# Two P times V back to back every eight tiles, scores in stretches of three, in a fused attention and gated-adapter kernel

## The reference

```
xn = layernorm(x)
q = (xn @ Wq.T + bq) * scaling              # 16 heads x 16
k, v = split(xn @ Wkv.T + bkv)              # one head of 16 each
w = softmax(qr @ k.T)                       # per batch 16*512 rows, 512 keys
attn = (w @ v) @ Wo.T + bo
...
logits = x @ w_gate                         # adapter: best of 6 experts by gate
attn = softmax(x @ tokens.T * C ** -0.5)
delta = ((attn @ val + x) @ wd_w.T + wd_b) * scale
out = log(sum(exp(delta) * gates))
...
x = x + attn_branch(xn) + ffn_branch(xn)
```

## Time and profile before

| | |
|---|---|
| Median of 3 runs | 902.43 us (899.44 to 903.38) |
| The profiled execution | 902.32 us, its span 900.4 us |
| PE busy | 857.9 us, 95% of the span |
| DVE busy | 780.2 us, 87% |
| ACT busy | 674.6 us, 75% |
| POOL busy | 512.7 us, 57% |
| Chain that ended last | PE 79%, DVE 15%, issue 3% |

### The profile page before, as it was taken

The page is one execution under the profiler, slowest core; times in us unless marked ns, Lnnn a source line. Parts: engine busy times, 40 slices in busy tenths (PEclk is TensorE's granted clock), DMA queues, the critical chain, the costliest instruction groups (busy, mean ns, idle before and its releaser), DMA issues.

```text
span 900.4 us, 17856 instructions
## 1 busy us (share of the span) xinstructions
PE 857.9 (95%) x5913; PEld 288.0 (32%) x5913; DVE 780.2 (87%) x1489; ACT 674.6 (75%) x1370; POOL 512.7 (57%) x691
## 2 busy tenths in 40 slices
PE   7779999999999999999999999999999999999988
PEld 5332232323323232332323333233333323232223
DVE  7698898989989898998989898898989889898935
ACT  3117887877878787787878778787787878887884
POOL 3764566665556666565666656566664656635210
PEclk8688999999999999999999999999999999999999
DMA  4431343434344343534435353443435334241212
GB/s 129 105 69 37 105 81 95 108 101 119 85 107 101 97 112 97 118 86 118 89 97 113 96 119 85 118 95 92 113 95 119 85 118 92 74 111 50 63 59 72
DMA packets 125073, 86.06 MB, mean 96 GB/s; under 512 B 57143, under 2 KB 109112, under 8 KB 124984
## 3 DMA queue, kind: packets, MB, share of 16 engines
q1 hardware_dynamic: 124824, 84.82, 38.2%
q10 hardware_dynamic: 160, 0.10, 0.0%
HBM read 39.30 MB, written 33.54 MB: 81 GB/s over the span
## 4 chain that ended last, share of the span: by engine, by line
PE 79%; DVE 15%; issue 3%; ACT 1%; POOL 1%; DMA 1%; SPq 0%; DVEq 0%
PE pO L373 25%; PE pA L355 19%; DVE M L829 9%; PE pB L360 8%; PE pA L496 5%; PE pA L443 5%; PE pA L514 4%; PE pA L498 3%; PE pA L432 2%; PE pA L468 2%; PE pA L483 2%; DVE st L749 2%; PE pB L476 1%; ACT P L648 1%; PE pB L454 1%
## 5 line engine op out<-in xcount | busy, mean ns | idle before, releaser
L829 DVE TENSOR_REDUCE M<-pA 128x1 f32<-128x512 f32 x1024 | 651.9, 681 | 80.1 <-PE pA L355 76.0
L648 ACT ACTIVATE P<-pB 128x512 f32<-128x512 f32 x1002 | 555.4, 603 | 133.2 <-PE pB L360 129.6
L355 PE MATMUL pA<-K,Q 48*128 48x512 f16 x1024 | 324.6, 388 | 25.1 <-DVE M L829 9.8
L360 PE MATMUL pB<-Q,K 50*128 50x512 f16 x1002 | 317.5, 385 | 0.3 <-DVE M L829 0.3
L373 PE MATMUL pO<-P,VK 128*32 128x512 f32 x2048 | 273.5, 606 | 2.1 <-ACT OTr L654 1.1
L355 PEld LDWEIGHTS pA<-K,Q 48*128 48x128 f16 x1024 | 67.8, 94 | 344.7 <-DVE M L829 285.1
L975 POOL TENSOR_SCALAR Cz<-Cx 128x512 f32<-128x512 f32 x32 | 62.1, 1941 | 38.6 <-ACT Cx L630 38.6
L373 PEld LDWEIGHTS pO<-P,VK 128*32 128x32 f32 x2048 | 40.5, 108 | 99.2 <-issue 66.2
L514 PE MATMUL pA<-wo,On 128*128 128x256 f32 x246 | 70.2, 407 | 0.0
L360 PEld LDWEIGHTS pB<-Q,K 50*128 50x128 f16 x1002 | 64.0, 94 | 7.4 <-ACT P L648 5.5
L960 POOL TENSOR_SCALAR Ms<-M 128x32 f32<-128x32 f32 x32 | 9.7, 303 | 97.5 <-DVE M L829 97.5
(11 more groups left out here) (156 smaller groups left out, 807.8 us busy)
## 6 DMA issues: line engine op xcount, KB each, us to landing
o_parts<-OTr SPq DMA_DIRECT2D x62, 256.0 KB, 2.3
X<-in_x SPq DMA_DIRECT2D x16, 512.0 KB, 3.9
q_pieces<-Qp SPq DMA_DIRECT2D x64, 128.0 KB
out<-OUT SPq DMA_DIRECT2D x32, 256.0 KB, 3.4
Op<-o_parts SPq DMA_DIRECT2D x31, 256.0 KB
Rb<-l_parts SPq DMA_DIRECT2D x31, 256.0 KB
Q<-q_pieces SPq DMA_DIRECT2D x30, 256.0 KB, 4.5
Q<-q_pieces SPq DMA_DIRECT2D x34, 128.0 KB, 4.6
```

The costliest lines, as they stand in the source:

```text
L355: e.matmul(bank1("ab", t)[:, :], Q16[r:r + 48, b % 3, h, 128 * s:128 * s + 128], K16[r:r + 48, b % 3, :], start=True, stop=True).then_inc( ...
L360: e.matmul(bankB(t)[:, :], K16[r:r + 50, b % 3, 128 * i:128 * i + 128], Q16[r:r + 50, b % 3, :, 32 * hh:32 * hh + 32], start=True, stop=Tr ...
L648: e.activation(P[:, u % PR, :], bankB(u + LB)[:, :], ACT.Exp, scale=alpha).then_inc(S("e"))
L829: e.tensor_reduce(M[:, t // 32 % 2, t % 2, t % 32 // 2:t % 32 // 2 + 1], bank1("ab", t)[:, :], AX, ALU.max, negate=True).then_inc(S("mx"))
```

## The change

The distance of P times V, the stretches of pairs and the ring are changed, in `slots()` and one constant:

```diff
-PR = 12
+PR = 16
...
     for n in range(NT + LB):
-        put("ab", n - n % 2 + 0.02 * (n % 2) if n < NT else n - n % 4 + 0.02 * (n % 4), n)
+        put("ab", n - n % 8 + (0, 0.02, 0.04, 3.3, 3.32, 3.34, 6, 6.02)[n % 8] if n < NT else n - n % 4 + 0.02 * (n % 4), n)
...
     for v in range(NT // 4):
-        put("pv", 4 * (v + LV + (v + LV >= NT // 4)) + 1, v)
+        if v + LV < NT // 4:
+            put("pv", 8 * ((v + LV) // 2) + 5.6 + 0.1 * (v % 2), v)
+        else:
+            put("pv", 4 * (v + LV + (v + LV >= NT // 4)) + 1, v)
```

## The result

The changed kernel takes **1008.79 us** (median of 4, 1006.19 to 1010.44) against 900.93 us for the kernel before in the same session: ratio 1.119, 95% interval 1.117 to 1.121. The forecast was 971 us in a range of 924 to 1000. The sign held, and so did the waits that it worked out; the clock, which it had put at nothing, is what takes the time out of the range.

The account below looks back on a forecast made before the run. PE bounds the kernel: 50.5 us a batch without waits, less 1.9 for joins, plus 8.4 of bank waits gives 57.0 against 52.39. Over about 14.5 batches +67, last batch +2: 902.3 + 69 = 971 us, range 924 to 1000.

Parts of the forecast that it names:

- What bounds the kernel, and the joins: PE sets the pace, 50.5 us a batch without waits; joining two P times V saves 1.9 us a batch.
- Stretches of three and fillers in pB: The third score pair behind five pB fillers a batch waits for a conversion on ACT: 5.3 us a batch.
- What comes on top, worked: Further bank waits in the filler windows, worked: 3.1 of 8.4 us, giving a batch of 57.0 us.
- From a batch to the kernel: About 14.5 batches, 4.6 us more each: +67 us; start and tail within 3 us, last batch +2.
- The clock falls: PE at half clock around the L461 window in a third to all batches: 990 to 1020 us, chance 0.15.
- Its price: Cost of the clock falling: 3.5 us at half clock, 1.2 to 3.5 us a batch, 990 to 1020 us.
- The rule named beside that rival: Skill text: PE idling briefly between matmul groups cycling through banks swings the clock; by it, falling clock would be the forecast.
- The smaller rival: Only the five pB filler waits count, slack takes up the rest: 53.9 us a batch, 925 us, chance 0.14.
- the faster one: pB banks come back in time, so only the joined P times V count: 875 us, chance 0.04.
- The ring at nothing: P gets 16 slots in place of 12 for the later P times V; costed at nothing.

Follow-up runs that it names:

- e1: The changed kernel with the four conversions of pB fillers moved on ACT ahead of the exponential of the tile following the filler: 941.1 us, ratio 1.044.
- e3: Only the stretches of three, three and two, with P times V one by one as in the kernel before: 976.8 us, ratio 1.083.
- e11: The changed kernel with 2 to 4 extra matmuls over all 128 rows in PE's holes ahead of five pairs a batch: 977.7 us, ratio 1.085.
- e6: The changed kernel with the ring of exponentials at 12 slots, as before the change: 1009.5 us, ratio 1.119.
- e4: The changed kernel with the pair of tile 5 moved behind the two P times V, so stretches of three, two, three: 932.7 us, ratio 1.036.
- e5: The changed kernel with 2 to 5 extra matmuls of 48 rows in PE's holes ahead of five pairs a batch: 988.9 us, ratio 1.096.

## Why the prediction was wrong in size, point by point

- **What bounds the kernel, and the joins:** right. The joined form takes 1.85 us as in the single case of the tail.
- **Stretches of three and fillers in pB:** right to 0.02 us in four windows of five. The third pair behind L457 came after 1.55 us (1.53 was forecast), behind L464 after 1.37 (1.39), L479 1.68 (1.66), L499 with L507 1.71 (1.69). Behind L517 with L507 it came after 1.46 (1.32), held by DVE's maximum and not by MT; the 0.3 us added by hand for DVE there make up for it. e1 shows that the place of the four conversions on ACT is the cause, e3 that it needs no join.
- **What comes on top, worked:** right. A batch at full clock takes 57.07 us (57.0).
- **From a batch to the kernel:** 67 us for the batches; with the middle at full clock (e11) tiles 64 to 960 take 66.4 us more than before. The ends were off: 4.4 us more up to tile 64 and 5.5 us more behind tile 960, where I had put 2 in all.
- **The rival "The clock falls", chance 0.15:** this is the step that failed. The sum of 971 us holds nothing for the clock; it cost 31 us (e11). With the 8 us at the ends that makes up the miss of 38 us. I set the fall aside since "the holes are shorter (0.4 to 1.0 us)" than the 1.35 us of the earlier trace rows. Holes of 0.92 and 0.49 us in one stretch of 3.40 us, with PE busy for 1.61, stood right ahead of a fall; I had even counted 1.9 of 3.8 us busy there, close to the 1.77 of 3.40 of the earlier trace rows, and let one row's hole outweigh it. The sign that I had named for this rival, a granted clock under 1 in the middle, is what came.
- **Its price:** 990 to 1020 us holds the measured time, in part by luck. I took 3.5 us a fall and at most one fall a batch. A fall cost 1.66 us, since 3.4 us at half clock still do the work of 1.7, and there were five falls in four batches.
- **The rule named beside that rival:** the Trainium skill (TensorE: Matmul & The Clock Gate, A second HAM failure mode: psum-queue depth-cycling) describes a clock that swings where PE idles briefly between groups of matmuls that cycle through banks. These traces agree in part. The change has 15 falls in the middle, behind holes of at most 0.92 us, while e3, whose third pairs come as late, has none.
- **The smaller rival and the faster one:** both wrong. The slack of earlier windows took up nothing.
- **The ring at nothing:** right (e6).

## What to carry to other kernels

When work is regrouped on an engine that issues in order, go through the banks and ask of each group's last member whose conversion frees its bank, and what that conversion stands behind on its own engine; here one place on ACT was worth 7% of the kernel. Then put a price on the clock for the holes that are left, short ones too: here falls of 1.66 us each came behind holes of 0.9 us, in one order and not in another, and only the trace told which. Where the time is set by chains of this kind, moving a step is safe only if all that waits for it, on every engine and on the DMA queue, has time left or is moved with it.

## What was not expected of the hardware

- In the middle of the change the clock fell behind holes of at most 0.92 us, and never behind the longest one, of 1.09 us. In e4 it fell in six of 13 batches that were alike up to that place; why in these is open.
- In e5 it fell even behind a stretch in which PE was busy 2.66 of 3.30 us, much of it with matmuls of 48 rows. With the same holes filled by matmuls of 128 rows (e11) there was no fall, though PE was about as busy: 2.64 us in its least busy 3.40 us (166.6 to 170.0 us), against 2.59 in e5 (223.3 to 226.7). The two runs differ in the rows and in the count of these matmuls (17 against 15 a batch), fewer in the run without falls. Why the one keeps the clock and the other doesn't stays open.
- Two P times V back to back: the second takes 0.86 us (two passes of 0.43), where a single one, with what surrounds it, takes 1.00 and 0.08 ahead of it.
